# A four-layer graph network on one core: the edges of the first 1024 nodes kept as 64-node rows of seven fields

## The reference

```python
x = ln(x + L0(x))   # wx = x @ W.T + b; temp = segsum(vals[:,None] * wx[src], dst); wx * temp
                    # vals = where(dst != src, w, 0) ** 2
x = ln(x + L1(x))   # agg = segsum(concat(x[src], edge_attr) @ W1 + b1, dst); concat(x, agg) @ W2 + b2
x = ln(x + L2(x))   # two weighted SAGE layers: segsum(w/deg * x[src], dst) / deg, twice
x = ln(x + L3(x))   # three steps: t[k] = h @ W_et[k].T + b_et[k]
                    # a = segsum(t[etype, src], dst); h = gru(a, h); then a gate and a value
```

## Time and profile before

| | us |
|---|---|
| median of 3 runs | 13733.29 (13729.97 to 13739.07) |
| the profiled execution's span | 15388.9 |
| PE / DVE / POOL / ACT busy in it | 9965.8 / 6792.6 / 9707.6 / 1404.0 |
| DMA packets, bytes | 4070001, 2778.79 MB |

### The profile page before, as it was taken

One profiled execution on the slowest core, in us unless ns is written; L12 is line 12 of the kernel. 1 busy time (PEld: TensorE's weight loads), 2 busy tenths in 40 slices (PEclk: granted clock), 3 DMA queues, 4 the chain that ended last, 5 costly groups with the idle time before them and its releaser, 6 DMA issues. The chain is left out here.

```text
span 15388.9 us, 172841 instructions
## 1 busy us (share of the span) xinstructions
PE 9965.8 (65%) x37130; PEld 6375.4 (41%) x37131; DVE 6792.6 (44%) x20397; ACT 1404.0 (9%) x4108; POOL 9707.6 (63%) x8863
## 2 busy tenths in 40 slices
PE   6777774444466666555545555588876888677775
PEld 4444444334335444334333333344443444334443
DVE  3333333333367775666656666333332333222223
ACT  1111111111100000000000000100000000000001
POOL 3888887777746666566655555366665666566662
PEclk7555556667787787667767677799997999889887
DMA  8888887777687775677747666477775777467773
GB/s 276 198 198 195 198 180 146 163 162 128 101 223 196 192 193 137 173 192 194 191 125 185 180 180 177 147 210 215 212 195 140 214 212 209 136 183 193 192 191 90
DMA packets 4070001, 2778.79 MB, mean 181 GB/s; under 512 B 430093, under 2 KB 3820298, under 8 KB 4069630
## 3 DMA queue, kind: packets, MB, share of 16 engines
q1 hardware_dynamic: 3529604, 2147.73, 50.7%
q0 software_dynamic: 508368, 612.97, 21.0%
q10 hardware_dynamic: 31722, 15.04, 0.3%
HBM read 2025.54 MB, written 778.19 MB: 182 GB/s over the span
## 5 line engine op out<-in xcount | busy, mean ns | idle before, releaser
L1012 POOL DMA_INDIRECT ring<-t_types,stage x3408 | 3273.1, 960 | 2164.6 <-issue 1349.2
L1012 POOL DMA_INDIRECT ring<-t_x,stage x2272 | 2213.4, 974 | 1450.6 <-issue 887.6
L1544 PE MATMUL bank<-work 128*128 128x512 f32 x5216 | 2624.0, 647 | 596.7 <-DMA work<-t_types 241.1
L1566 PE MATMUL bank<-ring 128*128 128x128 f32 x13632 | 2260.0, 320 | 974.6 <-DMA ring<-t_types,stage 236.2
L1566 PEld LDWEIGHTS bank<-ring 128*128 128x128 f32 x13632 | 2102.0, 229 | 1754.9 <-issue 1461.1
L2032 DVE TENSOR_REDUCE work<-work 128x512 f32<-128x2048 f32 x524 | 1911.5, 3648 | 1012.6 <-DMA work<-t_pairs 931.0
L968 POOL DMA_INDIRECT t_sums<-ring,stage x1136 | 1766.0, 1555 | 432.1 <-issue 262.4
L2007 DVE TENSOR_TENSOR acc<-acc,bank 128x128 f32 x1704 | 480.9, 282 | 3267.0 <-remote 2074.2
L1544 PEld LDWEIGHTS bank<-work 128*128 128x128 f32 x5216 | 1035.5, 210 | 1734.9 <-issue 1378.9
L1012 POOL DMA_INDIRECT ring<-t_h,stage x1136 | 1080.1, 951 | 782.3 <-ACT stage L1214 407.5
L1549 PE MATMUL bank<-work 128*128 128x512 f32 x1048 | 733.6, 788 | 454.8 <-issue 273.3
(11 more groups left out here) (298 smaller groups left out, 11271.9 us busy)
## 6 DMA issues: line engine op xcount, KB each, us to landing
work<-t_pairs SPq DMA_DIRECT2D x2352, 512.0 KB
t_pairs<-acc SPq DMA_DIRECT2D x272, 740.0 KB
t_pairs<-acc SPq DMA_DIRECT2D x272, 370.0 KB
t_pairs<-acc SPq DMA_DIRECT2D x74, 1360.0 KB
work<-t_types SPq DMA_DIRECT2D x294, 256.0 KB
t_types<-work SPq DMA_DIRECT2D x144, 512.0 KB
ring<-t_types,stage POOLq DMA_INDIRECT x3408
ring<-t_x,stage POOLq DMA_INDIRECT x2272
```

What stands on the lines that cost most here:

```text
L1012: pool.indirect_dma_start(msg[:, u, :], None, table, bass.IndirectOffsetOnAxis(ap=stage[:, u:u + 1], axis=0)).then_inc(slot_dma[u], 16)
L1544: mm = pe.matmul(bank[4 + half][:, :], dense_t[:, tile, k_ * D:(k_ + 1) * D] if ph > 3 else dense_x[:, tile, :], dense_b[:, half, k_ * 4:( ...
L1566: mm = pe.matmul(bank[q][:, 0:P], msg[:, u, :], hot[:, u, :], start=k_ == 0, stop=k_ == K - 1)
```

## The change

It does five things.

1. The tables' layout. There are 16 windows of 64 nodes in place of eight of 128, and 440 chunks in place of 432 (110 groups). A row belongs to one source and one window and has seven fields of 64: one for each type's count, the number of edges, the sum of weights, and the sum of squared weights without self-loops (1792 B). The first eight of the 16 windows' places are in `t_pairs0`, the others in `t_pairs1`. The cold part still has 71 turns with this input.
2. The hot stage handles chunks, not groups. They come from four streams (chunks 0 to 110, 111 to 221, 222 to 331, 332 to 439), one of each in a "tick". A chunk is one accumulating DMA of 1792 B rows, and it waits only for the last DMA of its own stream. There are no more messages, no `t_wx` rows and no scatters to `t_sums` here. PE spreads the keys into PSUM from one line. The features' sums (hot_feat) are added a tick later, from the same bank.
3. The first layer's hot part moves to the l0 pass. For each of 98 tiles of destinations SP loads the squared-weight field of both tables (two DMAs of 256 KB in pieces of 256 B), PE transposes eight blocks, ACT copies them, and PE multiplies them by the hot nodes' `t_wx`. Two of the four sums are added by DVE instead of PE.
4. The untyped passes read one field: 128x512 a unit in pieces of 256 B (256 KB where it was 1 MB), one matmul a unit, and the adding up of types is gone. The typed passes read four fields of a row together, in pieces of 1 KB where it was 512 B, with the same bytes and matmuls. 16 windows are added at a pass's end.
5. All zeros are written in the cold part: 272 times two pieces of 663.6 KB, where it was 740 and 370 KB, and none in the hot stage.

The core of the diff:

```diff
-WINDOWS = (0, 39, 55, 67, 77, 86, 94, 102)
-HG = 108
+HALF = P // 2
+WINDOWS = (0, 111, 158, 193, 222, 248, 272, 294, 314, 332, 350, 366, 382, 398, 413, 426)
+HG = 110
+STREAMS = (0, 111, 222, 332, HG * K)
+FULL = KT + 3
+ROW = FULL * HALF
...
-                        zero_piece(BT[0], (t * NQ + (q - NQ)) * (P * ZA), ZA, 5)
-                        zero_piece(BT[1], (t * NQ + (q - NQ)) * (P * ZB), ZB, 2)
+                        for h in range(NH):
+                            zero_piece(BT[h], (t * NQ + (q - NQ)) * (P * ZA), ZA, 4)
...
+            def hot_scatter(j, ticks, following):
+                for k, streams in enumerate(ticks):
+                    go(hot_staged, j * K + (k + 1))
+                    for s in range(streams):
+                        u = k * HB + s
+                        if k or not isinstance(j, int) or j:
+                            go(hot_dma[s], j * (K * 16) + k * 16)
+                        pool.indirect_dma_start(PAIR_ROWS[TABLE_OF[s]], ..., pair_out[:, u, :], None,
+                                                compute_op=ALU.add).then_inc(hot_dma[s], 16)
...
+            def hot_prods(j, ticks, following):
+                        if k or not isinstance(j, int) or j:
+                            pe.wait_ge(hot_kept, hot_chunk(j, k - 1, s, ticks))
+                            pe.wait_ge(hot_feat_added, hot_chunk(j, k - 1, s, ticks))
+                        pe.wait_ge(hot_pairs, hot_chunk(j, k, s, ticks))
+                        pe.matmul(o[:, 0:ROW], pair_eqs[:, r, :], pair_hot[:, r, :], start=True, stop=True)
+                        pe.matmul(o[0:DE + 1, ROW:ROW + HALF], hot_rec[:, k * HB + s, :],
+                                  pair_hot[:, r, F_ONE * HALF:(F_ONE + 1) * HALF], start=True, stop=True)
...
+            def mix_rows(at, tiles):
+                for a in range(tiles):
+                    wait(sp, mix_turned, (at.g - 2) * A + a + 1)
+                    for h in range(NH):
+                        sp.dma_start(mix_in[...], PAIR_BLOCKS[h][..., F_W0 * HALF:(F_W0 + 1) * HALF])
+            def mix_turn(at, a):
+                for i in range(BLOCKS // 2):
+                    mm = pe.transpose(bank[2 + a % TR * 2 + i // 4][...], mix_in[...], ident[:, :])
+            def mix_prod(at, a):
+                for i in range(BLOCKS // 2):
+                    mm = pe.matmul(bank[at.par][:, a * P:(a + 1) * P], mix_slot(a)[...], hot_wx[:, i, :], ...)
...
-                for k in range(0, KT * 4, 8):
-                    sp.dma_start(dense_b[:, half, k:k + 8, :], PAIR_BLOCKS[half][at, k:k + 8, int(ph in (2, 3)), :])
+                if ph > 3:
+                    wait(sp, dense_done, unit - 1)
+                    sp.dma_start(dense_b[:, half, :, :], PAIR_BLOCKS[half][at, :, 0:KT * HALF])
+                else:
+                    wait(sp, dense_done, unit + (1 - NH * TILES) ...)
+                    sp.dma_start(dense_w[:, c, :, :], PAIR_BLOCKS[half][at, :, field:field + HALF])
...
-                    v.tensor_reduce(dense_sum[:, c % TILES, :], dense_b[:, half, :, :].rearrange("p (k b) c -> p (b c) k", k=KT),
-                                    AXIS.X, ALU.add).then_inc(types_summed, 1)
```

More of the change, by code:

```diff
@@ L213, in place @@
             return v if by is None else v.rearrange("p (a b) -> p a b", b=by)
[L215 removed]
+        zero_rows = place(acc, 0, GN)
         first_key = place(acc, half, FC, I32)[0:FP, :]
@@ L547, in rows_in, with pass_rows @@
                     sp.dma_start(by_tile(slot[:, at.i, :]), rows(t, at.g)).then_inc(d.ld[at.i], 16)
-            def pass_rows(d, left, loads, store, last=1, ph=None):
+            def pass_rows(d, left, loads, store, last=1, ph=None, more=None):
                 if ph is not None:
@@ L624, in _ @@
             sp.wait_ge(attr_out, 32)
-            sp.wait_ge(staged, PS)
             sp.wait_ge(kept_act, FIELDS * K // 2 + 1)
-            hot_node_rows(0)
-            with turns(sp, 1, SPLIT) as t:
-                hot_node_rows(t, zeros=True)
-            with turns(sp, SPLIT, HTURNS) as t:
-                hot_node_rows(t)
+            for i, w in enumerate(PLACES):
+                node = loaded(sp.engine, window_i[0:1, w:w + 1], 1, HOT - HALF, "the kernel bounds a hot group's first node")[0]
+                sp.dma_start(hot_wx[i % 2 * HALF:(i % 2 + 1) * HALF, i // 2, :], WX[bass.ds(node, HALF), :]).then_inc(hot_wx_in, 16)
@@ L933, in _ @@
                 pool.dma_start(t, a[0:HE].rearrange("(g e) -> g e", e=GE)).then_inc(groups_in, 16)
-            for lo, hi in zip(WINDOWS, WINDOWS[1:] + (HG,)):
-                pool.dma_start(hot_tile_i[lo:hi, :], S_DST[lo * GE:lo * GE + 1].rearrange("(a e) -> a e", a=1).to_broadcast([hi - lo, 1])
-                               ).then_inc(groups_in, 16)
+            with nc.allow_non_contiguous_dma(reason="the first nodes of the hot windows, one element each"):
+                for i, c in enumerate(WINDOWS):
+                    pool.dma_start(window_i[0:HG, i:i + 1], S_DST[c * P:c * P + 1].rearrange("(a e) -> a e", a=1).to_broadcast([HG, 1])
+                                   ).then_inc(groups_in, 16)
             go(hot_made, 1)
@@ L1259, in step_root, with mix_keep, l0_step @@
                 return part
-            groups(act, lambda at: root(p_l0, at))
+            def mix_keep(g, a):
+                n = g * A + a
+                act.wait_ge(mix_turned, n + 1)
+                wait(act, mix_done, n + (1 - TR))
+                for two in range(2):
+                    ins = act.activation(mix_slot(a)[:, two * 4 * P:(two + 1) * 4 * P], bank[2 + a % 2 * 2 + two][:, :], ACT.Copy)
+                ins.then_inc(mix_kept, 1)
+            def l0_step(at):
+                for a in range(LAST_TILES if at.last else A):
+                    mix_keep(at.g, a)
+                if not at.first:
+                    root(p_l0, at.plus(-1))
+            groups(act, l0_step)
+            root(p_l0, LAST)
             stage_pass(1, meta_src, 0, {0: rows_turned(True), 2: step_root()})
@@ L1974, in hot_feat_add, with hot_feat_adds @@
-            def hot_feat_add(g):
-                node = loaded(v.engine, cols(hot_row, g, 1), 1, HOT - P, "the kernel bounds a hot group's first node")[0]
-                v.wait_ge(hot_feat_prod, g + 1)
-                wait(v, hot_feat_added, g)
-                into = hot_feat[0:DE + 1, bass.ds(node, P)]
-                v.tensor_tensor(into, into, bank[1][0:DE + 1, 0:P], ALU.add).then_inc(hot_feat_added, 1)
+            def hot_feat_adds(j, k, ticks):
+                streams = ticks[k]
+                node = loaded(v.engine, cols(hot_row, j * (K * HB) + k * HB, streams), streams, HOT - HALF,
+                              "the kernel bounds a hot chunk's first node")
+                for s in range(streams):
+                    n = hot_chunk(j, k, s, ticks)
+                    v.wait_ge(hot_kept, n)
+                    wait(v, hot_feat_added, n - 1)
+                    into = hot_feat[0:DE + 1, bass.ds(node[s], HALF)]
+                    v.tensor_tensor(into, into, bank[HB + s][0:DE + 1, ROW:ROW + HALF], ALU.add).then_inc(hot_feat_added, 1)
@@ L2068, in gather_steps @@
                 v.wait_ge(added, (SURE - 1) * NQ + ((ph - 1) * ADDS + 1))
[L2069 to L2072 removed]
+                for i, w in enumerate(PLACES):
+                    node = loaded(v.engine, window_i[0:1, w:w + 1], 1, HOT - HALF, "the kernel bounds a hot group's first node")[0]
+                    into = acc[:, bass.ds(node, HALF)]
+                    link(v.tensor_tensor(into, into, bank[4 + i // NB][:, i % NB * HALF:(i % NB + 1) * HALF], ALU.add))
                 def last_sums(t):
```

534 lines of the change are left out of this document (271 added, 263 removed).

## The result

The changed kernel takes 13134.74 us (median; 13133.42 to 13136.43), the kernel before, beside it, 13731.63 us. The ratio is 0.9566, with a 95% interval of 0.9555 to 0.9577: 597 us less, where 1112 less were forecast. The sign was right; the time lies above the range's end of 13080.

The account below looks back on a forecast made before the run. POOL's DMA issue was taken to bound scatter and hot stage, with waits above its floor in the passes. -908 + 257 - 560 - 90 + 20 + 30 = -1251: 14138 for 15388.9 profiled, scaled to 12620 us; 8-in-10 range 12250 to 13080.

Parts of the forecast that it names:

- Hot stage: 440 accumulating DMAs in place of 864, near POOL's floor of 818 us: 900 us, so -908 us.
- The landing: Hot stage: time for a stream's last DMA of 1792 B rows to land, put at 3 to 5 us, with 5.9 available.
- The l0 pass: New 256 B loads, PE transposes and products, and copies raise the pass from 173 to 430 us: +257 (+180 to +530).
- DMA is the later one: l0 pass: DMA's 423 us outlast PE's 352 at the high clock, so the pass takes 430 us.
- The untyped passes: Without adding up types and with lighter loads, three passes take 4795 us for 5355: -560 us (bounds -915 and nothing).
- each has 270 to 400 us above POOL's floor: All six gather passes: time above the 1420 us POOL needs for 1136 gathers; in untyped ones, mostly waits for ACT's index copy.
- The typed passes: Same bytes and matmuls with half the packets: -90 us (0 to -200).
- Cold scatter and the rest: Larger zero pieces in the cold scatter +20 us (0 to +150); set-up's small loads and copies, and more windows per pass, +30.
- The scaling: Whole kernel: the median is 0.892 of the profiled span, so 14138 us was scaled evenly to 12620 us.
- The stalls stay: Rival, 20%: POOL's waits in the untyped passes remain, so these give 150 us in place of 560; 12980 us.
- The low clock: Rival, 15%: PE stays at the low clock and paces the hot stage (1144 us) and l0 pass (700); 13080 us.
- The landing of the wide rows: Rival, 4%: 1792 B rows of one stream land one after another, slower than before from 19.6 us; 13970 at 22 us.

Follow-up runs that it names:

- narrow rows: Changed kernel with 256 of 448 columns in each accumulating DMA of the hot stage: 14835.36 us beside 15393.62 for the kernel before; hot stage 925 us.
- short matmul: Changed kernel with the hot stage's matmul cut from 448 to 128 columns: 14772.73 us beside 15393.62 for the kernel before; hot stage 877 us.
- loads alone: Changed kernel making all mix-row loads in the l0 pass, without their transposes, copies and products: 14692.42 us beside 15393.62 for the kernel before, ratio 0.9537.
- work alone: Changed kernel with all the mix's work in the l0 pass but loads of two groups only: 14634.36 us beside 15393.62 for the kernel before, ratio 0.9511.
- level B: Slower of two levels that executions fell on: the kernel before takes 15394 to 15556 us there, against 13728 to 13750 on the other.
- b_light: Kernel before, untyped passes with a quarter of the dense loads and a copy for the type sum: 13738.3 us, ratio 0.9993; repeated as b_light_2: 15419.64 us, ratio 0.9907.

## Why the prediction was wrong

- **Hot stage: right.** -908 with a stage of 900; it was -897 with 921. The landing is 4.4 to 6.2 us (median 5.2), a little above the 3 to 5 taken. One size was off: the 1792 B row costs 0.873 × 16 × 900 / 61781 = 203 ns (GpSimd's queue in the changed kernel, 2400:3300, below) where a straight line gave 151. The narrow rows show that this cost nothing. Of the 100 us above the floor, the short matmul gives 30 to 55 to the path through PE; the rest is open.

```profile
q0 software_dynamic: 61781, 96.97, 87.3%
```

- **The l0 pass: both costs right, their overlap wrong.** +257 taken, +358 measured, inside the bounds of +180 to +530. The two terms came out: 423 us taken for the DMA engines and 399 measured with the loads alone, 352 taken for PE at the high clock and 348 measured with the work alone. The piece's time was taken too low (22.8 ns for 19.4), but the loads alone still stay under their 423 us, so it explains none of the 101 us. The step that failed is "DMA is the later one", the assumption that loads and TensorE's work overlap. SP issues the mix rows behind a wait for the variance of a group that TensorE has just finished, so they partly take turns: 533 us together, 412 with the issue moved. The prediction says nowhere what SP waits for ahead of these loads.
- **The untyped passes: wrong, the main error.** -560 taken, -91 measured (of which 49 are the first pass). The failed step is "each has 270 to 400 us above POOL's floor", taken from the earlier trace rows as a property of the kernel. It is one of level B. In the executions that were timed the passes ran within 75 us of GpSimd's pace before and after; at level B the excess is there in both kernels, so its cause is not the one that I gave it either. b_light and b_light_2 show both. Most of the 91 us lie in two passes of the table above: 46 in the first, of which b_light got 5, and 35 in the third, of which it got 28. What the other 41 of the first are due to is not shown.
- **The typed passes: wrong in the same step.** -90 taken, -9 measured.
- **Cold scatter and the rest: right in the first, 27 us too much in the second.** +20 and +30 taken; +22 and about +3 measured. GpSimd's DMA takes 2142 / 1136 = 1.89 us for 1.87, at a DMA share of 0.90 (the rule of three gave 0.95).
- **The scaling: wrong.** "No row says where the difference lies, so I scale evenly" took 1251 × 0.108 = 135 us off the gain, though the hot stage and the l0 pass don't differ between the two executions. Two things in the profile did say where: the 1656 us are 276 a pass, most of the excess over GpSimd's floor (267 to 397 a stage), while the cold scatter stood at its floor already; and ACT's and SP's waits for "remote", 4295.5 us of ACT's in the six passes, had no explanation in the kernel. Had I put the passes at 1420 plus their ends, the other terms as they stand, unscaled, give -908 + 257 + 20 + 30 = -601, or 13132 us. That it meets 13134.74 so closely is luck: the l0 pass is 101 us dearer, and the passes gained 100.
- **The rivals.** "The stalls stay" (20%) came nearest in its main term (91 us against its 150), though for another reason; with the same l0 term and the same scaling it gave 12980, 155 us too low. The low clock did not come: 0.77 in the hot stage and 0.81 in the l0 pass. The landing of the wide rows was never near 19.6 us a tick; POOL waits 39.8 us in all for t_pairs in this group of the changed kernel:

```profile
L1047 POOL DMA_INDIRECT t_pairs<-acc,pair_stage x440 | 688.9, 1566 | 231.8 <-ACT pair_stage L1241 98.4 <-issue 93.6 <-DMA t_pairs<-acc,pair_stage 39.8
```

- The page "DMA: Bandwidth & Descriptors" of the Trainium skill, section "Specifications", asks for 512 B and has a read-modify-write below it. The runs agree in the sign: per byte a 256 B piece takes 22.8 / 30.0 × 2 = 1.52 times as long as a 512 B one. It is not as dear as the 512 B one, by which I had 571 us for the pass: the loads alone take 399. No run shows whether a read-modify-write is the reason.

## What to carry to other kernels

Where a profiled execution is longer than the median, find the stages that hold the difference before reading any wait in it: compare each stage with the floor of the engine that paces it, and look for idle time that the profile gives to nothing in the kernel. A stall in such a stage is not a gain to be booked until a cheap experiment (here: a quarter of the loads and no sum) has shown that it yields. And where a new load has an unchanged consumer in the same pass, read which wait its queue makes just ahead of it; loads and work that each fit can still take turns, and moving one issue ahead of the wait was worth 107 us here (137 at level B).

## What the runs showed of the hardware

- The same program has two levels, 13.73 to 13.75 ms and 15.39 to 15.56 ms, with all executions taken together on one of them. The excess lies in the gather passes, with joint stops of four engines, about 8 us in the stretch shown. Its cause is open.
- The time of a packet of an accumulating indirect DMA, averaged over all packets of the queue, is 81 ns with 512 B rows (cold scatter), 0.560 × 16 × 870 / 59280 = 131 ns with 1024 B rows (narrow rows) and 203 ns with 1792 B rows, the last two in the hot stage of the changed kernel. It depends on the stage too: by the trace's records a 1024 B packet took 125 ns in the hot stage before, at a DMA share of 0.74, and 145 ns with the narrow rows. My 109 ns for 1 KB came from the former.
- GpSimd's time for such a DMA hardly depends on the row: 1.55 us at 512 B and 1.57 us at 1792 and 1024 B.
- Cutting TensorE's columns by half in a stage where it takes turns with others (128 for 448 in one of its matmuls) went with a granted clock of 0.50, its lower level of 1.2 GHz, for 0.76, a mean between the two levels: the matmul of 448 columns took 722 ns at the one, the one of 128 columns 501 ns at the other.
